# One step of a hand-written order moved: where a macro's answers are returned among the first experts

## The reference

```python
for _ in range(ITERS):                       # 2
    ctx = concatenate([integrated, v])
    shared_ctrl = gelu(ctx @ shared_w1 + b) @ shared_w2 + b
    ctrl = experts(ctx, idx, ...)            # two of 8 experts per token
    # a, b, g = split(ctrl, 3)
    # v' = sigmoid(a) * v - softplus(b) * (x - mu);  x' = x + 0.1 * sigmoid(g) * v'
    halt = sigmoid(gelu(integrated @ halt_w1 + b) @ halt_w2 + b)
    integrated, v = each + halt * (mixture of shared and routed answers - each)
refined = gelu(integrated @ refine_w1 + b) @ refine_w2 + b
out = x + integration_weight * refined
```

## Time and profile before

| what | value |
|---|---|
| three runs | 3391.64, 3406.15, 3433.51 us (median 3406.15) |
| the profiled execution | 3376.8 us, its span 3375.1 us |
| busy: PE, DVE, ACT, POOL | 2913.8, 2560.1, 1876.2, 1104.7 us |
| mean granted clock of PE | 0.937 |
| first experts' rounds | about 950 to 1650 us of the span |

### The profile page before, as it was taken

The page is one execution under the profiler, slowest core; times in us unless marked ns, Lnnn a source line. Parts: engine busy times, 40 slices in busy tenths (PEclk is TensorE's granted clock), DMA queues, the critical chain, the costliest instruction groups (busy, mean ns, idle before and its releaser), DMA issues.

```text
span 3375.1 us, 99419 instructions
## 1 busy us (share of the span) xinstructions
PE 2913.8 (86%) x42634; PEld 1914.3 (57%) x42634; DVE 2560.1 (76%) x5230; ACT 1876.2 (56%) x3255; POOL 1104.7 (33%) x1294
## 2 busy tenths in 40 slices
PE   6999999998468988988569999999999998599994
PEld 4555555664245555555326565666556566388873
DVE  4677777675748888888657999899999896477774
ACT  3444444444357888888345666656656554166651
POOL 1333333221711222221232443343443332255552
PEclk7999999999789999999778999999999998599996
DMA  7476879100154333342200000000000000156666
GB/s 284 185 281 233 308 289 190 47 2 2 45 179 134 128 126 126 129 135 65 75 1 3 9 11 10 11 13 10 11 10 10 11 13 12 71 211 219 225 221 172
DMA packets 161608, 355.76 MB, mean 105 GB/s; under 512 B 13821, under 2 KB 98559, under 8 KB 154896
## 3 DMA queue, kind: packets, MB, share of 16 engines
q1 hardware_dynamic: 147088, 323.95, 28.2%
q0 software_dynamic: 14080, 25.45, 2.3%
HBM read 136.33 MB, written 216.67 MB: 105 GB/s over the span
## 4 chain that ended last, share of the span: by engine, by line
PE 51%; DVE 25%; ACT 14%; issue 5%; DMA 2%; SPq 1%; POOL 1%; DVEq 0%; POOLq 0%; ACTq 0%
PE ps L1558 6%; PE ps L135 5%; PE ps L137 4%; PE ps L136 4%; PE ps L905 2%; PE ps L346 2%; DVE t L494 2%; ACT t L1044 2%; ACT t L1042 2%; PE ps L912 2%; PE ps L350 2%; PE ps L301 2%; PE ps L307 2%; PE ps L331 2%; DVE t L531 2%
## 5 line engine op out<-in xcount | busy, mean ns | idle before, releaser
L1558 PE MATMUL ps<-t 128*128 128x512 f32 x608 | 325.9, 652 | 56.9 <-DVE t L2072 25.8
L245 POOL TENSOR_SCALAR_AFFINE_SELECT t<-t 128x512 f32<-128x512 f32 x256 | 169.4, 662 | 568.8 <-ACT t L434 568.8
L434 ACT ACTIVATE t<-ps 128x768 f32<-128x768 f32 x256 | 207.1, 809 | 219.4 <-PE ps L333 219.4
L135 PE MATMUL ps<-t 128*128 128x512 f32 (+1 forms) x660 | 276.5, 419 | 36.9 <-DVE t L476 15.1
L494 DVE TENSOR_REDUCE t<-ps 128x2 f32<-128x512 f32 (+1 forms) x512 | 260.4, 550 | 56.6 <-PE ps L307 56.4
L1370 POOL DMA_INDIRECT deltas<-t x92 | 94.4, 1026 | 508.4 <-DVE t L1316 486.3
L137 PE MATMUL ps<-t 128*128 128x512 f32 (+1 forms) x660 | 255.7, 387 | 0.0
L136 PE MATMUL ps<-t 128*128 128x512 f32 (+1 forms) x660 | 255.0, 386 | 0.0
L2825 POOL DMA_INDIRECT answers<-t x156 | 154.1, 988 | 160.0 <-DVE t L2796 122.1
L482 DVE SCALAR_TENSOR_TENSOR t<-t,ps 128x512 fp32r<-128x512 f32 x128 | 95.5, 746 | 129.1 <-ACT t L412 67.6
L1558 PEld LDWEIGHTS ps<-t 128*128 128x128 f32 x608 | 105.0, 197 | 143.0 <-issue 54.5
(11 more groups left out here) (443 smaller groups left out, 8313.1 us busy)
## 6 DMA issues: line engine op xcount, KB each, us to landing
paired<-t SPq DMA_DIRECT2D x14, 8384.0 KB, 38.4
t<-experts SPq DMA_DIRECT2D x39, 1536.0 KB, 6.9
sorted<-t SPq DMA_DIRECT2D x22, 1950.0 KB, 8.9
t<-in_wP SPq DMA_DIRECT2D x92, 320.5 KB, 3.5
experts<-t SPq DMA_DIRECT2D x8, 1536.0 KB, 5.5
t<-sorted SPq DMA_DIRECT2D x39, 260.0 KB, 5.9
t<-answers SPq DMA_DIRECT2D x16, 512.0 KB, 6.9
t<-in_wE SPq DMA_DIRECT2D x8, 768.0 KB, 38.2
```

What stands on the lines that cost most here:

```text
L135: pe.e.matmul(out, a[0], b[0], start=start, stop=False, skip_group_check=True)
L245: pool.e.affine_select(own, own, [[0, 2], [0, 2], [1, 128]], ALU.is_ge, 0.0, base=0, channel_multiplier=-1).then_inc(*kept(b, j))
L434: act.e.activation(pt[:, p, :, :], ps[:, k:k + 2, 0:384], ACT.Exp, scale=float(8 ** -0.5)).then_inc(*prob(b, j))
L1558: pe.e.matmul(ps[out, k, :], lhs, rhs, start=True, stop=True).then_inc(*e_pe(u, name))
```

## The change

In a round, the step back (of macro n - 3) moves from ahead of bring (of macro n + 1) to behind the new macro's soft and the spread. The list is one for all engines, so the step moves in the queues of PE, DVE and POOL.

```diff
-                                (0 <= n - 3, "back", n - 3, 0), (n + 1 < MACROS, "bring", n + 1, 0),
-                                (now or last, "logs", n, 0), (now, "soft", n, 0),
-                                (n + 1 < MACROS, "spread", n + 1, 0), (last, "soft", n - 1, 1),
+                                (n + 1 < MACROS, "bring", n + 1, 0), (now or last, "logs", n, 0), (now, "soft", n, 0),
+                                (n + 1 < MACROS, "spread", n + 1, 0), (0 <= n - 3, "back", n - 3, 0),
+                                (last, "soft", n - 1, 1),
```

## The result

The changed kernel takes 3500.84 us (median, 3483.68 to 3530.48) against 3407.06 for the kernel before: a ratio of 1.0275, interval 1.0223 to 1.0328. It is 94 us slower; the forecast was 3503.

The account below looks back on a forecast made before the run. The loop was taken to be bound by a chain through ScalarE, one VectorE reduction and TensorE. Wait 66.5 plus clock 30.4 make 96.9 us, added as 97 to the 3406 median: 3503, 2.8% slower; range 3445 to 3540.

Parts of the forecast that it names:

- The reading of what bounds: The loop runs through ScalarE, one VectorE reduction and TensorE; the first L1238 hangs on ScalarE's logarithm, 1.61 us behind L1046.
- The new wait: On TensorE, L944 waits for the first spread copy, delaying the older control: 3.50 us in 19 macros, 66.5 us.
- The clock: TensorE's 4.7 us gap drops its clock, slowing L944, control and halts: 1.6 us in 19 macros, 30.4 us.
- the smaller bound: The clock loss of 1.6 us a macro, shown by two of three earlier gaps and taken for the forecast.
- a gap that stayed at full clock: Sign against the forecast: TensorE's gap before L944 keeping 2.4 GHz; no size given.
- the other bound: Clock loss of 2.9 us a macro, from the 3.89 us gap at 1626.78; kept for the range.
- No cost elsewhere: GpSimd's displaced scatters, SP's load (about 7 us of cover left) and the buffers cost nothing.
- The clock holds: Rival: TensorE stays at 2.4 GHz through the gap, so only the wait costs: 3473; chance 0.10.
- The clock falls deeper: Rival: TensorE's clock costs 2.9 us, 6.4 a macro with the wait: +122, 3528; chance 0.13.
- Partly absorbed: Rival: half of TensorE's 3.5 us wait is hidden, clock term 0.8: 48 us, 3455; chance 0.08.
- does not arise: Rival: L944's bank is released before it is needed, so no wait and the time stays 3406; chance 0.06.
- Faster: Rival: VectorE bounds the loop and its 2.4 us waits before L1316 get filled: 46 us, 3360; chance 0.03.

Follow-up runs that it names:

- filled kernel: The changed kernel with bring's second coefficient group computed five times over from macro 4 on, to fill TensorE's gap: ratio 1.0192, 32.33 us a round.
- spread first: The changed kernel with the spread also moved, directly behind bring and ahead of the new macro's softplus: ratio 0.9982, 29.05 us a round.
- the wait alone: The kernel before, in its own order, with the new macro's control matmuls made to wait for the first spread copy: ratio 1.0134, 30.72 us a round.
- the longer wait: The kernel before with the new macro's control matmuls held for the second spread copy: ratio 1.0279, 34.13 us a round.
- copies first: The changed kernel with VectorE's product L1247 behind the two spread copies instead of ahead of them: ratio 1.0275, 33.95 us a round.

## Why the prediction was right

**The reading of what bounds.** Right. The first L1238 still starts 1.61 us behind the start of L1046 (1275.39, 1277.00), with or without L1316 in front.

**The new wait.** Right in its place and its cause: L944 is released by L1232, 3.67 us behind the start of L1238, which is to the hundredth the 1279.56 - 1275.89 of the forecast. Its size was put at 3.50 us a round and is 3.28, shown by the filled kernel; 0.12 of the difference lies between L944 and the older control, forecast at 1.89 + 2.38 + 1.83 = 6.10 us and there 1270.71 - 1264.73 = 5.98 (the 2.38 was read behind a wait; right behind other matmuls the set takes 2.27), and 0.1 between the start of the older control and the tanh of its second set, 1287.04 - 1282.16 = 4.88 us in the earlier trace rows and 1275.49 - 1270.71 = 4.78 there. That the wait and the queue behind it are the cause is shown from both sides: spread first keeps the move and loses the wait, the wait alone has the wait and not the move.

**The clock.** Right that it falls in every changed round, and that it costs is shown by the filled kernel. The term was 1.6 us a round and is 1.88. The argument for taking the smaller bound was that a longer gap hides part of the slow time. It holds for one kind of round only. In the round at 1280.67 some 2.7 us of the slow time lie inside the gap, and L944 and control take 6.13 us against 1268.89 - 1264.73 = 4.16 in the filled kernel: 1.97 lost. In the round at 1314.98 the granted clock is 1.00 from 1310 to 1315. By the forecast's own words a gap that stayed at full clock would have been a sign against it; the clock fell right at its end instead, nothing was hidden, and the price, 5.80 - 4.16 = 1.64, is small because the slow time was short. The forecast had neither the two kinds nor the common length of 34.13. So the kind of cost was right, and that 1.6 was near was in part luck. At shorter gaps the price was the other bound: 2.99 in the longer wait (gap 2.8) and 34.13 - 31.19 = 2.94 in copies first once it has settled (gap 3.4), as in the row of 2.9. The terms' errors, -0.22 and +0.28, nearly cancel, which is luck too: 19 x 5.16 = 98 against 96.9.

**No cost elsewhere.** GpSimd's scatters are through at about 1292.4, a round earlier 1258.2, and SP's load that follows goes out at 1265.07 unheld: 7 us of cover, as estimated. Spread first and filled gap have the displaced scatters too, and spread first loses nothing by them. GpSimd's earlier bring did win VectorE half a microsecond (L1244 1.76 us in all 23, against a median of 2.28), off the chain.

**The rivals.** "The clock holds" is what the filled kernel shows: a ratio of 1.0192, where its price of 3473 would be 1.0197. "The clock falls deeper" is what the two kernels with shorter gaps show, and not the change. "Partly absorbed" would leave half of the 3.5 us, and 3.28 were measured; "does not arise" falls with L944's wait for L1232. "Faster" failed on its own point: VectorE's waiting before L1316 was of no worth to the loop.

## What to carry to other kernels

Before a step is moved in a list that several queues share, walk through the rings of buffers with the new order: a step inherits the release of whoever held its buffer before, and moving it past two takers can tie it to a copy on another engine, with everything queued behind it. Where TensorE comes to wait longer inside a loop, count the clock as a second price of the wait (here a gap of 2.2 us cost it in 2 rounds of 19, gaps of 2.8 us and more in every round). It isn't proportional to the gap, and shortening a long gap may win nothing until the gap is short enough, or filled, for the clock to hold. Repeating work that is idempotent into a bank that is being written anyway is a cheap probe for how much of a stall is the clock.

## What the hardware showed that I had not expected

The slow time at a gap came in two lengths, though TensorE worked without a pause from the gap's end on. From the windows: in the longer wait from about 1266.5 (0.91 over three microseconds is 0.5 of them slow) to 1273.3, in copies first from 1286.8 to 1293.6, in the changed kernel from 1278.0 to 1284.8, 6.8 us each time; in the changed kernel's next round 3.4 us, and in the wait alone about as much (control 1.6 us late in the round shown). What a gap costs is decided by how much of this lies behind it: 6.4, 6.2, 4.1 and 3.4 us, half of which is 3.2, 3.1, 2.1 and 1.7, against 2.99, 2.94, 1.97 and 1.64 us lost. The length of the gap alone decides neither: in the changed kernel both kinds of round have a gap of 4.50 us, and in the wait alone the clock fell at a gap of 2.20 us and of 2.22 and held at others of 2.20 and 2.22. Why, no run here shows.

A scatter issued by GpSimd took up to 2.23 us where it overlapped VectorE's L1244, against a median of 0.99 before; the mean of L1370 rose from 1026 to 1332 ns. In the changed kernel:

```profile
1286.87 1.76 DVE L1244 TENSOR_TENSOR t<-t 128x1536 f32<-128x1536 f32 x1
...
1287.26 2.23 POOL L1370 DMA_INDIRECT deltas<-t  x1 [0.30 <-issue]
```

The Trainium skill ("GPSIMD Engine Reference", section "Specifications") lists GpSimd's SBUF interfaces as shared with VectorE, with contention when a VectorE instruction has two SBUF inputs. L1244 is such an instruction, L1238, which reads PSUM and beside which a scatter took 1.0, is not; the rows agree, though no run here varied it alone. In the kernel before it was the other way round, GpSimd's bring addition beside L1244, and L1244 bore the cost.
